# Context attention started inside the banded stage, and the banded products taken in the other order

## What is computed

```python
x = x + _L1_attn_ref(_layernorm(x, axis=-1), L1_attn_wq, L1_attn_wk, L1_attn_wv, L1_attn_wo, L1_attn_q_norm_w, L1_attn_k_norm_w)
x = x + _L1_xattn_ref(_layernorm(x, axis=-1), ctx_1024, mask_BxS2_bf0, L1_xattn_Wq, L1_xattn_bq, L1_xattn_Wkv, L1_xattn_bkv, L1_xattn_Wout, L1_xattn_bout, 16)
x = x + _L1_ffn_ref(_layernorm(x, axis=-1), L1_ffn_w_gate, L1_ffn_w_up, L1_ffn_w_down)
# in _L1_attn_ref, 8 heads of 128, WINDOW = 16:
scores = jnp.einsum('bhqd,bhkd->bhqk', q, k) * scale + bias[None]
probs = jax.nn.softmax(scores, axis=-1)
y = jnp.einsum('bhqk,bhkd->bhqd', probs, v)
return y.transpose(0, 2, 1, 3).reshape(Bx, Tx, N_HEADS * HEAD_DIM) @ wo
# in _L1_xattn_ref, 16 heads of 8:
scores = jnp.einsum('bhid,bhjd->bhij', q, k) * scale
attn = jax.nn.softmax(jnp.where(mask[:, None, None, :], -jnp.inf, scores), axis=-1)
out = jnp.einsum('bhij,bhjd->bhid', attn, v).transpose(0, 2, 1, 3).reshape(b, sq, d) @ Wout + bout
```

## Time and profile before

| | |
|---|---|
| median of 3 runs | 1288.75 us (1281.43 to 1289.94) |
| profiled execution | 1287.54 us, its span 1285.7 us |
| PE busy | 1147.3 us (89%) |
| DVE busy | 918.7 us (71%) |
| ACT busy | 871.6 us (68%) |
| POOL busy | 616.9 us (48%) |
| mean granted TensorE clock | 0.95 of full speed |

### The profile page before, as it was taken

One profiled execution on the slowest core, in us unless ns is written; L12 is line 12 of the kernel. 1 busy time (PEld: TensorE's weight loads), 2 busy tenths in 40 slices (PEclk: granted clock), 3 DMA queues, 4 the chain that ended last, 5 costly groups with the idle time before them and its releaser, 6 DMA issues.

```text
span 1285.7 us, 17355 instructions
## 1 busy us (share of the span) xinstructions
PE 1147.3 (89%) x6235; PEld 607.0 (47%) x6235; DVE 918.7 (71%) x1768; ACT 871.6 (68%) x1126; POOL 616.9 (48%) x454
## 2 busy tenths in 40 slices
PE   5899999999999999986988898899989999975865
PEld 2444444444444444432333332477767777733544
DVE  5666667766766677757888888446648777688885
ACT  2799999999989998873667667656645666633311
POOL 3577777777766776794455444023320000054232
PEclk9999999999999999987889999899989999988878
DMA  7200000000000000010000000000010000000000
GB/s 182 59 1 1 1 1 1 1 1 1 1 1 1 1 1 1 14 54 6 13 1 1 1 1 2 1 1 1 1 62 1 1 2 1 1 1 1 0 9 25
DMA packets 25633, 14.51 MB, mean 11 GB/s; under 512 B 14558, under 2 KB 24396, under 8 KB 25420
## 3 DMA queue, kind: packets, MB, share of 16 engines
q1 hardware_dynamic: 25548, 13.39, 3.7%
HBM read 12.34 MB, written 1.05 MB: 10 GB/s over the span
## 4 chain that ended last, share of the span: by engine, by line
PE 34%; POOL 30%; issue 19%; DVE 14%; ACT 2%; POOLq 0%; DMA 0%; SPq 0%; ACTq 0%; DVEq 0%
DVE ARENA L1100 6%; POOL ARENA L2543 6%; POOL ARENA L2541 6%; POOL ARENA L2537 6%; PE PS L971 4%; POOL ARENA L2567 3%; POOL WQ L2554 3%; PE PS L1346 3%; PE PS L841 3%; PE PS L1335 2%; PE PS L1330 2%; PE PS L1322 2%; PE PS L945 2%; PE PS L773 2%; PE PS L789 2%
## 5 line engine op out<-in xcount | busy, mean ns | idle before, releaser
L2397 DVE TENSOR_SCALAR ARENA<-PS,ARENA 128x512 f32<-128x512 f32 x256 | 174.5, 744 | 65.8 <-PE PS L2031 65.7
L1100 DVE TENSOR_REDUCE ARENA<-PS 128x1 f32<-128x512 f32 x256 | 160.9, 683 | 27.8 <-PE PS L789 27.3
L1016 ACT ACTIVATE ARENA<-PS 128x1024 f32<-128x1024 f32 x128 | 128.8, 1025 | 62.0 <-PE PS L827 61.7
L2210 ACT ACTIVATE ARENA<-ARENA 128x2048 f32<-128x2048 f32 x64 | 122.2, 1912 | 61.3 <-DVE ARENA L2397 60.8
L2031 PE MATMUL PS<-ARENA 64*128 64x512 f32 x512 | 128.6, 621 | 0.0
L2217 ACT ACTIVATE ARENA<-ARENA,consts_sb 128x2048 f32<-128x2048 f32 x64 | 124.6, 1994 | 0.4
L2041 PE MATMUL PS<-ARENA 128*64 128x512 f32 x512 | 118.4, 605 | 1.3 <-issue 1.3
L2223 ACT ACTIVATE ARENA<-ARENA 128x2048 f32<-128x2048 f32 x64 | 118.3, 1897 | 0.0
L1281 POOL TENSOR_TENSOR ARENA<-ARENA 128x512 f32<-128x512 f32 x32 | 40.7, 1271 | 121.5 <-DVE ARENA L1239 121.0
L2550 POOL TENSOR_SCALAR WQ<-ARENA,consts_sb 128x512 bf16<-128x512 f32 x32 | 22.1, 692 | 159.6 <-DVE ARENA L2373 159.6
L789 PE MATMUL PS<-ARENA 32*128 32x512 bf16 x256 | 73.8, 413 | 25.1 <-DVE ARENA L1100 20.0
(11 more groups left out here) (292 smaller groups left out, 2673.8 us busy)
## 6 DMA issues: line engine op xcount, KB each, us to landing
ARENA<-in_window_bias_dram SPq DMA_DIRECT2D x1, 1536.0 KB, 6.4
WKVG<-in_L_attn_W_in_dram SPq DMA_DIRECT2D x3, 448.0 KB, 5.5
X<-in_x_dram SPq DMA_DIRECT2D x4, 256.0 KB, 4.5
W<-in_L_ffn_w_dram SPq DMA_DIRECT2D x1, 1024.0 KB
out_dram<-X SPq DMA_DIRECT2D x4, 256.0 KB, 2.3
BV<-in_L_attn_b_in_dram SPq DMA_DIRECT2D x1, 512.0 KB, 6.4
Wout<-in_L_attn_W_out_dram SPq DMA_DIRECT2D x1, 512.0 KB, 4.8
WQ<-in_L_attn_wq_dram SPq DMA_DIRECT2D x1, 512.0 KB, 3.4
```

The lines of the kernel that those rows point to most:

```text
L1016: act.activation(PT[m % PT_SLOTS], bank(("cP", m)), ACT.Exp, scale=0.5).then_inc(sem("c_exp"), 1)
L1100: dve.tensor_reduce(NMX[:, w % 2, t, h:h + 1], bank(("cS", n, j)), AX.X, ALU.max, negate=True).then_inc(sem("c_max"), 1)
L2210: act.activation(chunk(u, half), chunk(u, half), ACT.Sqrt).then_inc(sem("rooted"), 1)
L2397: dve.tensor_scalar(D[:, u % 2, kt, hd, :], bank(("S", u, c)), K2[:, u % 2, kt, hd:hd + 1], 1e-30, ALU.add, ALU.max).then_inc(sem("guarded ...
```

## The change

*Products in the other order.* A tile no longer multiplies its keys by NVO1. PE first weighs the normalized keys themselves, keys as the stationary operand and 4 heads of turned weights as 4 x nq moving columns, two products a tile ("dZ"). ACT copies the lower four heads out (`d_z_low`), DVE the upper four (`d_z_high`), into ZT. The product with NVO1 is then taken for several tiles at once: 8 products of 352 columns when three tiles of a batch are through, 8 of 160 when all five are (`project_out`). The keys have to lie with tokens as rows: for the first and last tile Y has them so, for the other three PE turns them ("dX") and ACT copies them (KTOK). V1 and its copy on DVE are gone.

*Set-up drawn ahead.* Keys and values of the context are made at tile step 2, the queries of batches 0 and 1 at tile steps 11 and 16. The values take one bank and one DVE add for all four batches. The fourfold copy of the context and the spreading of keys and values over heads move from DVE to POOL, all eight in a row. Tiles of the context stage move to memory that is free by then (W1, W2, weights of the earlier stages).

*Last tiles in the context's steps.* The banded loop ends at n = 17. What is left of tiles 17 to 19, the projection, the turn out, the layernorms of batches 2 and 3 and their queries are done at set steps s of the context's loop (table `ETAIL`), in which PE's order within a step is: the rest of the banded stage, scores of tile s + 2, turn of tile s - 2, values or output. There the two stages have banks of their own (DT: 0 to 3, E3: 4 to 6, O: 7) up to step 4, then E7: 0 to 6 and O: 7. Scores and exponentials share seven buffers, the exponential works in place. The turn out of a batch comes one tile step later than before.

```diff
-    b, ti = divmod(n - 1, len(TILES1))
+    b, ti = divmod(n - 2, len(TILES1))
     return b - 1 if ti == 0 and 1 <= b < B else None
+
+
+PARTS1 = ((0, 352, 3), (352, 512, 5))
+
+
+def projected(n):
+
+    b, ti = divmod(n, len(TILES1))
+    if ti == 4:
+        return b, 0
+    return (b - 1, 1) if ti == 1 and b else None
...
+BODY1 = B * len(TILES1) - 2
+CONTEXT_AT = 2
+QUERIES_AT = (11, 16)
+
+
+ETAIL = {"weigh18": 0, "weigh19": 2, "queries2": 3, "weigh_end": 4, "project": 6, "turn_out": 7, "rstd": 8, "normal": 9,
+         "turn": 10, "queries3": 11}
...
+def scores_at(s):
+
+    if s == ETAIL["turn"]:
+        return ()
+    if s == ETAIL["queries3"]:
+        return (s + 1, s + 2)
+    return (s + 2,) if s + 2 < B * QT else ()
...
+    def pool_at(s):
+        return "E3" if s <= ETAIL["weigh_end"] else "E7"
...
+        def context(pe, begin, done):
+
+            pe.wait_ge(sem("e_weights_in"), 16 * 6)
+            o = begin(("eK", 0))
+            done(pe.matmul(o[:, 0:P], EW["k"], CTXT[:], start=True, stop=True), ("eK", 0))
+            pe.wait_ge(sem("e_ctx4"), 1)
+            o = begin(("eV", 0))
+            for b in range(B):
+                mm = pe.matmul(o[:, b * P:(b + 1) * P], CT4[:, b], EW["v"], start=True, stop=True)
+            done(mm, ("eV", 0))
...
+            def turn_keys(b):
+                pe.wait_ge(sem("xt_ready"), norm_no(3, b))
+                o = begin(("dX", b))
+                for i in range(3):
+                    k0 = TILES1[i + 1][2]
+                    mm = pe.transpose(o[:, i * P:(i + 1) * P], XT[:, b, k0:k0 + P], ident)
+                done(mm, ("dX", b))
...
-                o = begin(("dV", n))
+
+            def finish(n):
+
+                b, ti = divmod(n, len(TILES1))
+                nq = TILES1[ti][1]
+                pe.wait_ge(sem("d_pt"), n + 1)
+                pe.wait_ge(sem("d_keys"), b + 1)
+                keys = Y[:, b, 0, :] if ti == 0 else Y[:, b, QT - 1, :] if ti == 4 else KTOK[:, b % 2, ti - 1, :]
+                o = begin(("dZ", n))
                 for half in range(2):
-                    mm = pe.matmul(o[:, half, :], XT[:, b, k0:k0 + P], NVO1[:, half * 512:(half + 1) * 512],
-                                   start=True, stop=True)
-                done(mm, ("dV", n))
-
-            def finish(n):
-                b, ti = divmod(n, len(TILES1))
-                q0, nq, k0, _ = TILES1[ti]
-                pe.wait_ge(sem("d_pt"), n + 1)
-                pe.wait_ge(sem("d_v"), n + 1)
-                o = begin(("dO", b)) if ti == 0 else bank(("dO", b))
+                    mm = pe.matmul(o[:, half, 0:4 * nq].rearrange("p (h q) -> p h q", h=4), keys,
+                                   PT1[:, n % 2, 4 * half:4 * half + 4, 0:nq], start=True, stop=True)
+                done(mm, ("dZ", n))
+
+            def project_out(b, part):
+
+                q0, q1, tiles = PARTS1[part]
+                for name in ("d_z_low", "d_z_high"):
+                    pe.wait_ge(sem(name), len(TILES1) * b + tiles)
+                o = begin(("dO", b)) if part == 0 else bank(("dO", b))
                 for h in range(HD1):
-                    mm = pe.matmul(o[:, q0:q0 + nq], V1[:, n % 4, h * P:(h + 1) * P], PT1[:, n % 2, h, 0:nq],
-                                   start=ti == 0 and h == 0, stop=ti == len(TILES1) - 1 and h == HD1 - 1)
-                if ti == len(TILES1) - 1:
+                    mm = pe.matmul(o[:, q0:q1], NVO1[:, h * P:(h + 1) * P], ZT[:, b % 2, h, q0:q1],
+                                   start=part == 0 and h == 0, stop=part == 1 and h == HD1 - 1)
+                if part == 1:
...
+            for n in range(BODY1):
+                start(n + 2)
+                if projected(n) is not None:
+                    project_out(*projected(n))
+                if turned_out_batch(n) is not None:
+                    turn_out(turned_out_batch(n))
+                if n:
+                    finish(n - 1)
+                turn_weights(n)
+                if turn_next(n) is not None:
+                    ln_turn(4, turn_next(n))
+                if n == CONTEXT_AT:
+                    context(pe, begin, done)
+                if n in QUERIES_AT:
+                    queries1(pe, begin, done, QUERIES_AT.index(n))
+
+            def tail(s):
+                b = B - 1
+                if s == ETAIL["weigh18"]:
+                    finish(BODY1 - 1)
+                    turn_weights(BODY1)
+                if s == ETAIL["weigh19"]:
+                    project_out(b, 0)
+                    finish(BODY1)
+                    turn_weights(BODY1 + 1)
+                    ln_turn(4, b - 1)
+                if s == ETAIL["queries2"]:
+                    queries1(pe, begin, done, b - 1)
+                if s == ETAIL["weigh_end"]:
+                    finish(BODY1 + 1)
+                if s == ETAIL["project"]:
+                    project_out(b, 1)
+                if s == ETAIL["turn_out"]:
+                    turn_out(b)
+                if s == ETAIL["turn"]:
+                    ln_turn(4, b)
+                if s == ETAIL["queries3"]:
+                    queries1(pe, begin, done, b)
+
+            return tail
...
+            def z_out(n):
+                b, ti = divmod(n, len(TILES1))
+                q0, nq = TILES1[ti][0:2]
+                full(act, ("dZ", n))
+                if b >= 2:
+                    full(act, ("dO", b - 2))
+                act.copy(ZT[:, b % 2, 0:4, q0:q0 + nq], bank(("dZ", n))[:, 0, 0:4 * nq].rearrange("p (h q) -> p h q", h=4)
+                         ).then_inc(sem("d_z_low"), 1)
...
-                full(dve, ("dV", n))
-                if n >= 4:
-                    summed(n - 4)
-                dve.tensor_copy(V1[:, n % 4], bank(("dV", n)).rearrange("p k c -> p (k c)")).then_inc(sem("d_v"), 1)
+
+            def z_out(n):
+                b, ti = divmod(n, len(TILES1))
+                q0, nq = TILES1[ti][0:2]
+                full(dve, ("dZ", n))
+                if b >= 2:
+                    full(dve, ("dO", b - 2))
+                dve.tensor_copy(ZT[:, b % 2, 4:8, q0:q0 + nq], bank(("dZ", n))[:, 1, 0:4 * nq].rearrange("p (h q) -> p h q", h=4)
+                                ).then_inc(sem("d_z_high"), 1)
...
+            def tail(s):
+                b = B - 1
+                if s == ETAIL["weigh18"]:
+                    weights(BODY1)
+                    z_out(BODY1 - 1)
+                if s == ETAIL["weigh19"]:
+                    weights(BODY1 + 1)
+                    normalize(4, b - 1)
+                    z_out(BODY1)
+                if s == ETAIL["weigh_end"] + 1:
+                    z_out(BODY1 + 1)
+                if s == ETAIL["turn_out"]:
+                    add_to_stream(3, b, ("out1", b))
+                    stats(4, b)
+                if s == ETAIL["normal"]:
+                    normalize(4, b)
...
+            for s in range(STEPS + 2):
+                d_tail(s)
+                for n in scores_at(s):
+                    scores(n)
+                if s < 2:
+                    continue
+                n = s - 2
                 b, t = divmod(n, QT)
-                if n + 4 < STEPS:
-                    scores(n + 4)
                 pe.wait_ge(sem("e_p"), n + 1)
...
+            pool.wait_ge(sem("e_k"), 1)
+            for b in range(B):
+                pool.tensor_tensor(KX[:, b], KTX[:, b].unsqueeze(1).to_broadcast([P, HX, CK]),
+                                   const("xhead").unsqueeze(2).to_broadcast([P, HX, CK]), ALU.mult).then_inc(sem("e_kx"), 1)
+            pool.wait_ge(sem("e_v4"), 1)
+            for b in range(B):
+                pool.tensor_tensor(VX[b], V4[:, b].unsqueeze(1).to_broadcast([P, 4, P]),
+                                   const("vhead").rearrange("p (g c) -> p g c", g=4), ALU.mult).then_inc(sem("e_vx"), 1)
```

348 lines of the change are left out of this document (186 added, 162 removed).

## The result

The changed kernel takes 1271.92 us (median of 4 runs, 1270.53 to 1272.73) against 1289.35 us before (median of 4 runs beside them); the ratio is 0.9872, with a 95% interval of 0.9851 to 0.9893. It is 1.3% faster, 17.4 us. Forecast were 1268.0 us and a range of 1256 to 1279.

What follows compares the result with a forecast made beforehand. PE was taken to bound the banded stage; the hand-over was latency, and PE waits in the context stage. From 1287.5 us, 9.6 (banded stage) and 9.9 (tail) came off: 1268.0 us, range 1256 to 1279.

Steps and rivals of the forecast that it cites:

- the second rival: Banded stage: ACT and DVE in strict order lead each tile, PE waits; only 2 us gained there, 1276 us; chance 0.12.
- Piece 1: Banded stage up to the head products of batch 1: 4.8 us shorter, between 1.4 and 7.4.
- piece 3: Banded stage from the head products of batch 3 to tile 19's maximum: 0.5 us shorter.
- Piece 2: Banded stage, batches 1 and 2: 3.3 us saved per batch, less the queries of batch 0; 5.8 us shorter.
- The blanket 1.5: Banded stage: 1.5 us taken off the 11.1 us gain for lumps that don't fill each other, leaving 9.6.
- Tail: Tile 19's maximum to the bias of score tile 12: 63.6 us becomes 53.7, a gain of 9.9 us.
- E step 2: Context loop: DVE waits about 1 us, as PE does the 352-column projection ahead of tile 18's weighted keys.
- the turn out: Context loop: DVE's add for batch 3 waits 5.5 us for this turn, behind the context values of batch 0.
- E steps 10 to 12: Context loop: score tile 12 waits 2.5 us for batch 3's queries, behind batch 1's values and batch 0's quantized turn.
- The tail flows: Rival: DVE's wait for batch 3's turned output is covered and the body gains its full 11 us; 1258 us; chance 0.13.
- Convoy in the banks: Rival: three shared banks in early context steps let one late copy hold the next score; body gain only, 1278; chance 0.10.
- Slower by the clock: Rival: PE granted 1.2 instead of 2.4 GHz behind tile 19's maximum, 75 us there; 1298 us in all; chance 0.05.

Runs made afterwards that it cites:

- earlier masks: Changed kernel with conversion and scaling of the context masks moved on DVE from tile step 2 to tile step 0: 1270.92 us.
- the other bank: Changed kernel with the turned output of batches 0 to 2 in the two banks of the sums, not among the six of the scores: 1271.54 us.
- the kernel with the order alone: Kernel before with weighted keys and projection in two parts over all 20 tiles, old context stage, nothing drawn ahead: 1288.61 us.

## Why the prediction was right, and where it was off

The time lies 4 us from the forecast and well within the range: 17.4 us were gained for 19.5. The mechanism held, but part of the nearness is luck, as said below.

*Bound of the body.* Right: PE busy 95% at 0.99, the second rival (ACT and DVE lead each tile) did not come. The prices held: start to start, the 352 columns of a projection took 4.73 us, the 160 columns 2.18, weighted keys of 448 columns 1.5 to 1.6, of 192 0.66. Piece 1 was 5.2 for 4.8, piece 3 1.3 for 0.5.

*Piece 2* was the term that was off: 5.8 against 2.75. I had PE's rows right and missed three waits of PE that the change makes: 0.74 within the head products of batch 1 (DVE is late by the masks), and 0.91 twice, as the head products take the bank in which the turned output waits for DVE's add. Together 2.6 of the missing 3.0; the runs with earlier masks and the other bank took out each of them. The blanket 1.5 that I took off for lumps, and the 1.2 by which pieces 1 and 3 were better than forecast, made up for it: the body's sum came out at 9.3 for 9.6, and that closeness is in part luck.

*Tail.* Sized at 53.7 us, measured 57.95, so it gave 5.6 us and not 9.9: this was the largest miss. By its terms: E step 2, 1.65 for 1; the turn out, 6.41 for 5.5; E steps 10 to 12, 3.72 for 2.5; these three are 2.8 us. The small gaps between DVE's operations come to 1.45 for the 0.6 that I called hand-overs. DVE's own work is 44.7 us for 44.1 with the stretched normalizes. Within it the three normalizes take 4.9 for 5.2, and the weights multiply beside POOL 2.06 for 1.23, which I had ruled out. Together these are the 4.25. All places were right, and all waits came out longer: I laid each out from rows at their undisturbed length, and a wait that stands behind four operations can collect what each of them is late; this last is my reading, and no run tests it.

The prediction left the weights multiply at its old length, since in the overlap at 1037 the cost lay on POOL. That reading was wrong: that multiply ran from 1035.17 to 1036.39 and did not meet POOL's add at all. What POOL's add met, starting 0.23 us behind it, was DVE's product of Y and RMS, two rows from 1037.34 to 1038.63. In the tail the multiply does meet POOL, and here the cost lies on DVE; at the next meeting it lies on POOL:

```profile
1109.17 1.05 POOL L1905 TENSOR_TENSOR ARENA<-ARENA 128x512 f32<-128x512 f32 x1 [23.50 <-DVE ARENA L1838]
...
1115.63 1.24 DVE L1686 TENSOR_TENSOR ARENA<-ARENA 48x1024 f32<-48x1024 f32 x1
1115.75 2.10 POOL L1899 TENSOR_TENSOR ARENA<-ARENA 128x512 f32<-128x512 f32 x1
```

At 1109 POOL starts first and keeps its 1.05 us; DVE's multiply, 0.07 us behind it, takes 2.06. At 1115 DVE starts first and keeps its 1.24; POOL, 0.12 us behind it, takes 2.10 for 1.05. In all three meetings (the one at 1037 with them) the later one ends 0.07 to 0.15 us earlier than it would if it had begun only when the first was through (1110.22 and 1.23 give 1111.45, and it ended at 1111.30).

The rule beside that sentence of the prediction (the Trainium skill, GPSIMD Engine Reference, Key points) agrees with it: GpSimd contends with VectorE instructions that have two SBUF inputs. The same place names a second kind that I had left out, instructions in a 2-port perf mode. Whether the conversion and the scaling of the masks ran in such a mode no row here shows.

*Behind score tile 12* I had written that nothing changes; 2.25 us went. The add for context batch 1 had waited 1.04 us for its product and waits no more. The other 1.2 lie behind the last add (70.8 us for 72.0), in a stretch that differs by as much between the profiles of this study. This term at nothing was wrong in the other direction than the tail and hid half of its miss in the total, which again is luck.

*The rivals.* The tail flows: no, 6.41 us of wait. Convoy in the banks: in E steps 0 to 4 (steps of the context's loop) PE waits for a bank twice, 0.18 and 0.59 us, and ahead of them once for 0.53. Slower by the clock: the tail was granted 0.88, far from the 73 us that this rival needed; but the kernel with the order alone is this rival nearly come true, with a tail of 73.5 us, by another way: 3.1 of the 9.9 us more are rows at the low clock (1.8 in the projection, 1.3 behind the add), and the rest is, by my reading, the projection's rows in a serial place and the add that stands a step later.

*What the sum could not see.* I added up a body and a tail as if each half of the change brought its own. The experiments show that alone neither half brings that: the new order, put at 9.6, is worth 1.1 from the anchor (by the medians not to be told from nothing), the drawing ahead, put at 9.9, is worth 8.5. Alone the new order takes 10.45 us off the body and adds 9.9 to the tail, and beside the drawing ahead it adds only 3.6 there. My sum was right for the pair alone. Why PE's clock then falls lower than in the kernel before (0.71 for 0.84 between the add for batch 3 and the first bias), which is part of the difference, stays open.

## What to carry to other kernels

Rows taken out of a stage are worth their time only where that engine bounds, and a shorter stage can be followed by a longer hand-over: price the hand-over too, with all that moved behind the stage's end and with the clock that PE has there, and look for work that can run beside it. Here the same edit was worth nothing alone and 8.7 us beside the other. Test the part that you blame by itself: batch 3's projection stood in the serial place, and taking it away made the kernel slower in both surroundings. Where a stage hands over to another, the order of one engine's queue around a long product is worth microseconds per move, but of the two waits taken out in the tail about half turned up at the next link (1.7 of 4.1 us, 2.2 of 3.7), so measure them together. Compare profiles from the first changed instruction and not from the start; 3 us of spread came from the part that nobody had touched.

## What the runs showed of the hardware that I had not expected

- A conversion of 128x128 elements on DVE takes 0.22 us, and 0.93 beside POOL's multiply of two SBUF operands; a scaling 0.23 and 0.98. Each loses some 0.7 us however short it is.
- Where an operation of DVE and one of POOL, each with two SBUF operands, met with a readable start, the one that started first kept its length and the later one was lengthened by about what was left of the first: DVE 2.06 us for 1.23 behind POOL, POOL 2.10 for 1.05 and 2.18 for 1.27 behind DVE. That looks like waiting and not like sharing. Which one pays is then a matter of 0.1 or 0.2 us of order.
- The normalize of a layernorm, four tiles of 128x128, takes 1.11 us, and 1.91 when POOL works beside it in the tail.
- PE's granted clock rises when its pauses are filled with products that nobody reads (0.83 to 0.91, the same eight rows 5.60 and 3.60 us), and this was worth nothing, because PE was not the late one.
